# Selected LSTM on one core: the last products of each column tile signal by themselves, and the verdict on the guess is a signal from TensorE's sequencer

## The reference, cut to what matters

```python
def step(carry, x_t):
    h, c = carry
    sel_in = jnp.concatenate([h, c, x_t], axis=-1)
    logits = sel_in @ W_sel.T + b_sel
    onehot = jax.nn.one_hot(jnp.argmax(logits, axis=-1), Sx, dtype=x_t.dtype)
    g_all = jnp.einsum('bi,sgi->bsg', x_t, W_ih) + jnp.einsum('bh,sgh->bsg', h, W_hh) + b_ih + b_hh
    g = jnp.einsum('bsg,bs->bg', g_all, onehot)
    h2, c2 = _lstm_activate(g, c)
    return ((h2, c2), h2)
```

## Time and profile before

| | us |
|---|---|
| median of 3 runs | 8070.95 |
| lowest and highest | 8069.72, 8077.84 |
| span of the profiled execution, first to last instruction | 8073.7 |
| TensorE matmuls busy | 5912.7 |
| VectorE busy | 3912.4 |
| ScalarE busy | 1002.2 |
| GpSimd busy | 945.9 |

### The profile page before, as it was taken

The page is one execution under the profiler, slowest core; times in us unless marked ns, Lnnn a source line. Parts: engine busy times, 40 slices in busy tenths (PEclk is TensorE's granted clock), DMA queues, the critical chain, the costliest instruction groups (busy, mean ns, idle before and its releaser), DMA issues. The chain is left out here.

```text
span 8073.7 us, 210686 instructions
## 1 busy us (share of the span) xinstructions
PE 5912.7 (73%) x65214; PEld 2869.1 (36%) x65215; DVE 3912.4 (48%) x19391; ACT 1002.2 (12%) x4031; POOL 945.9 (12%) x2829
## 2 busy tenths in 40 slices
PE   3458997778778777777777777777777777777776
PEld 3423445544444433333333333333333333333332
DVE  5432112455555555455554554555455555455544
ACT  0011003111111111111111111111111111111111
POOL 5702113000000000000000000000000000000000
PEclk6579998999999999999999999999999999999999
DMA  3210004322222210000000000000000000000000
GB/s 80 0 65 0 0 0 168 108 78 74 78 74 76 74 39 8 8 4 8 4 8 4 8 8 4 8 4 8 4 8 8 4 8 4 8 4 8 8 4 23
DMA packets 292937, 219.99 MB, mean 27 GB/s; under 512 B 137196, under 2 KB 268652, under 8 KB 290609
## 3 DMA queue, kind: packets, MB, share of 16 engines
q1 hardware_dynamic: 162612, 160.58, 5.9%
q10 hardware_dynamic: 106110, 59.01, 2.8%
q0 software_dynamic: 24192, 0.10, 0.9%
HBM read 160.28 MB, written 59.36 MB: 27 GB/s over the span
## 5 line engine op out<-in xcount | busy, mean ns | idle before, releaser
L1021 PE MATMUL ps<-WH,hparts 128*17 128x512 f16 x49760 | 3016.9, 380 | 1475.7 <-DVE hparts L865 1312.8
L1021 PEld LDWEIGHTS ps<-WH,hparts 128*17 128x17 f16 x49760 | 1344.5, 90 | 2816.7 <-DVE hparts L865 1929.1
L838 DVE STREAM_TRANSPOSE gateT<-ps 128x512 f32<-128x512 f32 x1250 | 895.7, 717 | 1639.5 <-PE ps L1056 1632.3
L1090 PE MATMUL ps<-WH 128*128 128x512 f16 x4970 | 1244.9, 381 | 0.0
L470 POOL COPY xT<-hfull 128x4 f32 x1250 | 238.2, 191 | 5712.5 <-DVE hparts L863 5712.5
L584 ACT ACTIVATE gateT<-gblk 128x16 f32 x1250 | 288.2, 231 | 3512.5 <-DVE pick L833 3460.7
L981 PE MATMUL ps<-O,Adj 128*128 128x512 f16 x3000 | 650.5, 380 | 77.2 <-DVEq L752 77.2
L1064 PE MATMUL ps<-xT,wih_next 128*128 x2048 | 501.1, 388 | 135.6 <-DMA wih_next<-in_w_ih 121.0
L1090 PEld LDWEIGHTS ps<-WH 128*128 128x128 f16 x4970 | 404.2, 97 | 418.8 <-issue 54.8
L588 ACT ACTIVATE acts<-gates 128x16 f32<-128x16 f32 x1250 | 269.2, 215 | 1755.9 <-DVE gates L842 1755.9
L828 DVE TENSOR_REDUCE lmax<-ps 1x1 f32<-1x4 f32 x1250 | 186.8, 149 | 618.8 <-PE ps L1019 618.8
(11 more groups left out here) (137 smaller groups left out, 4222.5 us busy)
## 6 DMA issues: line engine op xcount, KB each, us to landing
wih_next<-in_w_ih SPq DMA_DIRECT2D x256, 256.0 KB, 2.9
gblk<-gate_inputs ACTq DMA_DIRECT2D x48, 800.0 KB, 5.2
gate_inputs<-gx_next SPq DMA_DIRECT2D x64, 500.0 KB, 2.6
wst<-in_w_hh ACTq DMA_DIRECT2D x32, 512.0 KB, 7.3
wih<-in_w_ih SPq DMA_DIRECT2D x16, 1024.0 KB, 7.9
adjacency<-Adj SPq DMA_DIRECT2D x2, 6400.5 KB, 24.7
Adj<-adjacency SPq DMA_DIRECT2D x2, 6400.0 KB, 27.1
gate_inputs<-gstage SPq DMA_DIRECT2D x16, 500.0 KB, 6.1
```

Of the source, the lines that this page charges most:

```text
L838: dve.transpose(gateT[:, :, 0:32], gate_ps.rearrange("p (c q) -> p c q", q=32)).then_inc(turned, 1)
L1021: nc.tensor.matmul(gate_ps[32 * j:32 * j + 17, :], hparts[:, k, :], WH[:, s * KC + k, part, j, :], start=(k == 0 and part == 0), stop=(k = ...
L1090: nc.tensor.matmul(ps[:, 2, :], WH[:, 0, 0, 0, 0:P], WH[:, 0, 0, 0, :], start=True, stop=True)
```

## The change

The closing matmul and its word of PSUM go. The four matmuls that end the four column tiles of a pass (k = 3, second part) each increment a semaphore: `guess_mm` in the guessed pass, `gates_settled` in the second one. Where the guess was right there is no second pass, and TensorE's sequencer adds 4 to `gates_settled` itself, in the other arm of the comparison. VectorE waits ahead of the transpose for both, each at 4 times the number of the step, which takes one register value more (`n4`).

```diff
--- before.py
+++ after.py
@@ -170,7 +170,6 @@
         ps = ctx.enter_context(nc.psum_tensor("ps", [P, 8, 512], f32))
         gate_ps = ps[:, 0, :]
         logit_ps = ps[0:1, 1, 0:S]
-        seal_ps = ps[0:1, 2, 0:1]
         unit_ps = ps[:, 3, 0:TB]
 
 
@@ -248,7 +247,8 @@
         scatter_seen = sem("scatter_seen")
         stage_seen = sem("stage_seen")
         pick_seen = sem("pick_seen")
-        gates_mm = sem("gates_mm")
+        guess_mm = sem("guess_mm")
+        gates_settled = sem("gates_settled")
         turned = sem("turned")
         gx_set = sem("gx_set")
         gates_ready = sem("gates_ready")
@@ -832,9 +832,10 @@
                 dve.wait_ge(lmark_ready, n)
                 dve.tensor_reduce(pick[:, :], lmark[:, :], AX.X, ALU.max).then_inc(pick_ready, 1)
 
-            def cell(n, n2):
-
-                dve.wait_ge(gates_mm, n)
+            def cell(n, n2, n4):
+
+                dve.wait_ge(guess_mm, n4)
+                dve.wait_ge(gates_settled, n4)
                 dve.transpose(gateT[:, :, 0:32], gate_ps.rearrange("p (c q) -> p c q", q=32)).then_inc(turned, 1)
 
                 dve.wait_ge(turned, n)
@@ -877,7 +878,7 @@
 
             def step(t):
                 n = dve.snap(t + 1)
-                cell(n, dve.snap(t * 2 + 2))
+                cell(n, dve.snap(t * 2 + 2), dve.snap(t * 4 + 4))
                 logit_parts(n)
                 choose(dve.snap(t + 2))
                 return n
@@ -895,7 +896,7 @@
                                       ALU.mult, ALU.add).then_inc(unit_out, 1)
             with dve.Fori(CHUNKS * SUB, N - 1) as t:
                 step(t)
-            cell(N, 2 * N)
+            cell(N, 2 * N, 4 * N)
 
             for t in range(RT):
                 b = t % 2
@@ -1011,6 +1012,7 @@
             def products(s, n, first):
                 if first:
                     pe.wait_ge(h_ready, n)
+                done = guess_mm if first else gates_settled
                 for k in range(KC):
                     for part in range(2):
                         if first and k == 1 and part == 0:
@@ -1018,9 +1020,11 @@
                             pe.wait_ge(lpart_ready, n)
                             nc.tensor.matmul(logit_ps, ones[:, 0:1], lpart[:, :], start=True, stop=True).then_inc(logits_mm, 1)
                         for j in range(4):
-                            nc.tensor.matmul(gate_ps[32 * j:32 * j + 17, :], hparts[:, k, :], WH[:, s * KC + k, part, j, :],
-                                             start=(k == 0 and part == 0), stop=(k == KC - 1 and part == 1),
-                                             tile_position=(0, 32 * j))
+                            last = nc.tensor.matmul(gate_ps[32 * j:32 * j + 17, :], hparts[:, k, :], WH[:, s * KC + k, part, j, :],
+                                                    start=(k == 0 and part == 0), stop=(k == KC - 1 and part == 1),
+                                                    tile_position=(0, 32 * j))
+                            if k == KC - 1 and part == 1:
+                                last.then_inc(done, 1)
 
             def products_of(chosen, n, first):
 
@@ -1052,8 +1056,8 @@
                 pe.reg_load(chosen, pick[0:1, 0:1])
                 with pe.If_ne(chosen, guess):
                     products_of(chosen, n, False)
-
-                nc.tensor.matmul(seal_ps, hparts[:, 0, 0:1], hparts[:, 0, 0:1], start=True, stop=True).then_inc(gates_mm, 1)
+                with pe.Else():
+                    pe.sem_inc(gates_settled, 4)
 
             def unit(c, u, n, w_in):
```

## The result

The changed kernel takes 8113.11 us (median of 4 runs, 8110.09 to 8118.6) against 8074.19 us before (4 runs); the ratio is 1.0047, with a 95% interval of 1.0033 to 1.0062. It is 39 us slower, where 7 were forecast; the time lies 5 us above the upper end of the range. The profiled execution took 8113.66 us, its span is 8110.6 us, 3.1 us less; the span is 36.9 us above the one of before. The granted clock is 0.964 in both profiles.

The account below looks back on a forecast made before the run. The prediction took a chain of 1250 dependent time steps to bound the kernel. Terms of -37 (plain hits), +28 (misses) and +16 us (unit hits) summed to +7, a median of 8078 us, range 8038 to 8108.

Parts of the forecast that it names:

- What bounds the kernel, and the kinds of steps: Recurrence: a chain of 1250 dependent steps; guess right (hit) or wrong (miss, second pass, 305), with or without unit matmuls.
- Plain hits: 763 right-guess steps without unit matmuls: the sequencer's increment replaces the closing matmul, 0.05 us saved a step, 37 us gained.
- The second wait: VectorE ahead of the transpose: the wait for gates_settled becomes an event of its own, 0.06 to 0.07 us more.
- Rival A: Ahead of the transpose: the gates_settled wait rides on it, guess_mm is the event; sum -59 us, 8012 us, chance 0.12.
- Misses: 305 wrong-guess steps: the transpose starts 0.09 us later after the second pass, 28 us lost (15 to 40).
- I take 0.04: End of a wrong guess's second pass: queue of three more increments, put at 0.04 us out of 0 to 0.12.
- rival B: End of the second pass in 305 wrong-guess steps: four increments queue, 0.08 us; sum +19 us, 8090 us, chance 0.25.
- Unit hits: 182 right-guess steps with unit matmuls: the event delays TensorE's queue by 0.09 us each, 16 us lost (5 to 20).
- Rivals C and D: C: event dearer than 51 ns, +53 us, 8124, chance 0.06; D: closing matmul's going worth more, -43 us, 8028, chance 0.09.
- The sum and the range: Whole kernel: +7 us, median 8078 us; bounds of the sum -33 to +37, range 8038 to 8108 us.
- Edits at no cost: VectorE's third register value, the satisfied wait and the guessed pass's increments: covered by idle time, no cost.

Follow-up runs that it names:

- e1: Changed kernel, but only the last column tile's product of the four that end a pass increments; 8087.85 us, ratio to before 1.0017.
- e5: Changed kernel with two increments a pass, on the second and last column tile; 8100.62 us, ratio to before 1.0029.
- e10: Changed kernel with four increments in the guessed pass and, in the second, one on the last column tile adding 4; 8086.61 us, ratio to before 1.0019.
- e2: Changed kernel with the two waits ahead of the transpose swapped, gates_settled written first; 8031.04 us, ratio to before 0.9940.
- e3: Changed kernel with one increment a pass and the two waits swapped; 8001.78 us, ratio to before 0.9907.
- e6: Kernel before, with its closing matmul, plus four increments ending each pass on a semaphore nobody waits for; 8105.41 us, ratio 1.0038.
- e7: Kernel before, plus a sequencer increment nobody waits for in the arm of a right guess; 8180.21 us, ratio 1.0129.
- e4: e3 with the closing matmul back in the right-guess arm, in the 256 unit steps, instead of the sequencer's increment; 7988.87 us, ratio to before 0.9889.
- e8: Kernel before, closing matmul only in the right-guess arm; after a wrong guess the second pass's last product increments the same semaphore; 8074.81 us, ratio 0.9996.

## Why the prediction was wrong, point by point

**What bounds the kernel, and the kinds of steps: right.** The wait table of after names 763 plain hits on the sequencer, and each kind moved by an amount of its own.

**Plain hits: right to 0.01 us in the step, too high in the sum.** The step read gained 0.05 us (0.98 after the pick, as forecast). The mean gained 0.037, 28 us instead of 37, within the bounds of 23 to 53. In 135 of the 763 there was no gain: the sequencer's increment starts 0.867 us after the pick's end there and 0.822 in the rest (medians). Before, only 39 hits were late in this way. Why, no run here tells; e1, e5 and e10 have it too, with periods at 4.67 beside 4.63.

**The second wait: right.** The event is the second one written (L838, 1250 times), and it costs what rows 9 gave: e2 took 0.07 us off hits and misses alike, against 0.06 to 0.07. Rival A's kernel is e2 in effect, 82 us faster than the changed one; it was priced at 66 us less. The gain that I forecast for hits was 0.05 us where 0.11 lay ready (4.675 to 4.563 in e3). So the larger part of what the change could give was lost to the order of two lines.

**Misses: the term that failed.** "I take 0.04" for three increments in a queue was mis-sized: they cost 0.076. A miss lost 0.139 us from the products' end to the transpose where 0.09 stood, and with the rest of the period 305 misses lost 44 us instead of 28. Of these 16 us the queue is 11 (305 x 0.036); 4 are the landing and the event without a queue, 0.063 us in e1 where 0.05 stood. The step that failed is the choice between the ends. The row I leaned on, a closing matmul noticed 0.04 us later behind products, measured something else: no increment stood ahead of it there. The upper end I had from it, 0.12 for three, was too high, and the sum didn't carry it: its 0.13 us a miss allow only 0.08 of queue. With 0.12 the upper bound would have been 305 x 0.17 = 52 us for the misses and +49 in all, 8120, which holds the time measured, by a figure that was itself too large. "Nothing shows that the unit serves increments one at a time" was true of the rows read but was no reason for the middle. e1, e5 and e6 show that each adds 25 ns, whoever it is for, and e5's landings that the spread of the completions, which rival B counted against the queue, absorbs none of it. Rival B, with a queue of 0.07 us and more, was what happened, at 0.076; it had 0.25. The rule of the Trainium skill that I had set beside it ("TensorE: Matmul & The Clock Gate", "The cost: per-tile semaphore tail") gives 26 ns an increment, 0.08 us here, and these runs agree.

**Unit hits: right in the mechanism and nearly in the size.** 0.094 us each against 0.09, 17 us against 16; that these agree to a microsecond is partly luck, since the sorting moves some of the cost into the unit misses. e7 (0.11 us for the event) and e4 (18 us back, 0.10 us each) show the cause as forecast, the event in TensorE's queue ahead of the unit's branches.

**Rivals C and D: wrong.** The events are 51 ns in all 945 cases, each an increment of 4, and a miss gave back 8 ns (e8).

**The sum and the range.** -28 + 44 + 17 = +33 where -37 + 28 + 16 = +7 stood. The bounds of the sum reached +37; with 8071 as the starting point that was 8108. Measured were +39 on 8074. Of the missing 26 us 16 are the misses (11 of them the queue), 9 the hits without gain, 1 the units; and the three runs at hand gave a median 3 us below that of the four.

**Edits at no cost: right, with one limit.** The four increments of a guessed pass cost nothing (e10 against e1). In the changed kernel the last of them lands 0.077 us before the verdict (median of plain hits). Where the guess's wait is the event (e2), it needs 0.071 us more than the verdict's, so little of the cover is left, and four signals in the guessed pass come near to mattering (4.566 in e2, 4.563 in e3).

## What to carry to other kernels

Where several matmuls end a group together, let the last one alone signal: every other increment there stands in line ahead of the one that is waited for, even if nobody waits for it. It is free only where something later covers it. When an operation has two waits, write the one that comes last first, if the trace shows the second as an event, and look again after each edit of the values they are compared with. A matmul that "only signals" may be cheaper than the sequencer's own increment: compare what stands behind it on its queue.

## What the runs showed of the hardware that was not expected

- An increment by a matmul of TensorE puts back the ones behind it by 25 ns, across semaphores, on top of the 9 ns between the completions (0.121, 0.146, 0.197 us for 1, 2 and 4; 0.102 us for four idle ones ahead of the closing matmul's). One that adds 4 costs as one that adds 1.
- From the landing of the increment waited for to the transpose's start it is 0.023 us where the wait rides on it and 0.094 where the wait is an event ahead of it.
- An increment by TensorE's sequencer holds its queue for 0.11 us, although it is recorded with 51 ns; a load and a tiny matmul in its place hold it 0.10 us less (e4 against e3, 18 us over 181 hits).
- In the tail of the column-tiled products a closing matmul recorded with 165 ns cost 8 ns (0.058 us before, 0.050 in e8).
